# Cross-attention with a norm: v made one batch later and kept in PSUM, transposed contexts kept for four batches, contexts loaded flat for the bound

## The reference, cut to what matters

```python
# x: (16, 512, 512), ctx: (16, 120, 256); Wq (512,512), Wk, Wv (256,512)
q = x @ Wq + bq                       # (16, 512, 512)
k = ctx @ Wk + bk                     # (16, 120, 512)
v = ctx @ Wv + bv                     # (16, 120, 512)
w = softmax((q @ k^T) / sqrt(512), axis=1)    # over the 512 tokens
y = w @ v + x
out = (y - mean(y)) * rsqrt(var(y) + 1e-6) * gamma + beta
```

## Time and profile before

| | |
|---|---|
| median of 3 runs | 225.95 us (225.01 to 226.12) |
| the profiled execution | 226.4 us, span 224.6 us |
| PE busy | 193.4 us |
| DVE busy | 174.2 us |
| POOL busy | 167.6 us |
| ACT busy | 162.0 us |

### The profile page before, as it was taken

How to read it: one execution, slowest core, us unless ns; L and a number is a source line. 1 busy time by engine, 2 the same in 40 slices (tenths; PEclk the granted TensorE clock), 3 DMA queues, 4 the chain that set the end, 5 groups by cost and what they waited for, 6 DMA issues and landing times.

```text
span 224.6 us, 4180 instructions
## 1 busy us (share of the span) xinstructions
PE 193.4 (86%) x1168; PEld 119.5 (53%) x1168; DVE 174.2 (78%) x435; ACT 162.0 (72%) x343; POOL 167.6 (75%) x164
## 2 busy tenths in 40 slices
PE   5698599999999999999999999999999999988000
PEld 4554567656657564657474646565655556524000
DVE  0482855698989598879695988796968899869993
ACT  2426467589898788787887988887969897886610
POOL 1000000438999999999999999999999999999792
PEclk9799889999999999999999999999999999999755
DMA  5999966001464656373636473646455544040454
GB/s 152 303 233 327 352 240 233 0 4 53 181 228 171 188 209 210 144 245 150 235 161 220 175 232 163 223 172 220 175 209 187 198 177 187 0 190 0 188 211 163
DMA packets 11914, 41.04 MB, mean 183 GB/s; under 512 B 1022, under 2 KB 5886, under 8 KB 8062
## 3 DMA queue, kind: packets, MB, share of 16 engines
q1 hardware_dynamic: 11614, 40.37, 50.9%
q10 hardware_dynamic: 288, 0.52, 1.0%
HBM read 24.12 MB, written 16.78 MB: 182 GB/s over the span
## 4 chain that ended last, share of the span: by engine, by line
POOL 60%; issue 10%; DMA 9%; PE 7%; DVE 6%; ACT 2%; DVEq 1%; SPq 1%; POOLq 1%; ACTq 0%
POOL obuf L959 22%; POOL obuf L953 20%; DMA obuf<-in_ctx 7%; POOL rstd L986 6%; POOL v_part L946 6%; POOL square_mean L972 4%; PE g_ps L395 2%; DMA out<-obuf 2%; PE s_ps L425 2%; DVE obuf L822 1%; DVEq L78 1%; PE v_ps L384 1%; POOL var_eps L979 1%; POOL var_eps L976 1%; PE xT_ps L403 1%
## 5 line engine op out<-in xcount | busy, mean ns | idle before, releaser
L953 POOL TENSOR_TENSOR obuf<-obuf,gamma_all 128x512 f32<-128x512 f32 x44 | 57.8, 1338 | 1.5 <-ACT obuf L617 1.5
L425 PE MATMUL s_ps<-xT,gT 128*120 128x512 f32 x128 | 57.8, 593 | 1.1 <-ACT xT L554 1.1
L959 POOL TENSOR_TENSOR obuf<-obuf,beta_all 128x1536 f32<-128x1536 f32 (+1 forms) x16 | 51.8, 3238 | 1.2
L617 ACT ACTIVATE obuf<-xbuf,shift,rstd 128x512 f32<-128x512 f32 x44 | 32.7, 804 | 15.1 <-POOL shift L991 15.1
L417 PE MATMUL pv_ps<-v_part,prob_part 120*128 120x512 f16 x135 | 35.6, 380 | 3.0 <-issue 1.4
L425 PEld LDWEIGHTS s_ps<-xT,gT 128*120 128x120 f32 x128 | 23.2, 183 | 27.2 <-issue 21.1
L403 PEld LDWEIGHTS xT_ps<-ident,xbuf 128*128 128x128 f32 x256 | 30.0, 143 | 13.1 <-issue 8.1
L403 PE MATMUL xT_ps<-ident,xbuf 128*128 128x128 f32 x256 | 34.3, 278 | 1.8 <-ACT xT L554 1.4
L554 ACT ACTIVATE xT<-xT_ps 128x512 f32<-128x512 f32 x64 | 34.1, 584 | 1.3 <-PE xT_ps L403 1.3
L833 DVE SCALAR_TENSOR_TENSOR xbuf<-pv_ps,back_y,xbuf 128x512 f32<-128x512 f32 x45 | 32.4, 743 | 0.8 <-POOL shift L991 0.6
L946 POOL TENSOR_TENSOR v_part<-v_scaled,v_part 120x512 f16<-120x512 f32 x16 | 21.5, 1344 | 13.6 <-ACT v_part L587 13.1
(11 more groups left out here) (119 smaller groups left out, 260.2 us busy)
## 6 DMA issues: line engine op xcount, KB each, us to landing
xbuf<-in_x SPq DMA_DIRECT2D x16, 1024.0 KB, 4.8
out<-obuf SPq DMA_DIRECT2D x14, 1024.0 KB, 4.2
out<-obuf SPq DMA_DIRECT2D x8, 256.0 KB, 2.4
ctx_nat<-in_ctx SPq DMA_DIRECT2D x16, 120.0 KB, 4.2
obuf<-in_ctx SPq DMA_DIRECT2D x2, 960.0 KB, 14.9
wq_nat<-in_L_xattn_Wq SPq DMA_DIRECT2D x2, 512.0 KB, 8.6
wk_nat<-in_L_xattn_Wk SPq DMA_DIRECT2D x1, 512.0 KB, 5.7
wv<-in_L_xattn_Wv SPq DMA_DIRECT2D x1, 512.0 KB, 12.6
```

The source lines that it names most:

```text
L425: mm = pe.matmul(s_ps[0:M, :], gT[:, k % 2, e, :], xT[:, e, :], start=(e == 0), stop=(e == EC - 1))
L617: act.activation(obuf[:, k % 2, j, :], xbuf[:, kn, j, :], ACT.Identity, bias=shift[:, j:j + 1], scale=rstd[:, k % 2, j:j + 1]).then_inc(no ...
L953: pool.tensor_tensor(obuf[:, k % 2, j, :], obuf[:, k % 2, j, :], gamma_all[:], ALU.mult)\
L959: done = pool.tensor_tensor(obuf[:, k % 2, 0:share, :], obuf[:, k % 2, 0:share, :], beta_all[:].unsqueeze(1).broadcast_to([P, share, E]), ...
```

## The change

v of batch b is made in slot b, no longer in slot b-1. It stays in its PSUM bank (v_ps; pv_ps[0] for batch 0): DVE scales it in place (`scale_v`), ACT takes the high half out of PSUM, behind `probs_to_high`, and DVE takes the low half (`v_to_low`), behind `probs_to_low`. POOL has no part in v. `ctxT` has four places. PE's product 2 waits for `v_low` where it waited for `v_copied`. `key_bias` of batches 1 and 2 moves into slot 1, and the low half of Wv behind `key_bias` of batch 0. `ctx_all` is loaded as one flat block over 128 partitions, 15,360 bytes in each, in two transfers (2048 and 1792 columns); ACT adds up two parts of 1024 columns, DVE two of 1024 and 768, and the last two of DVE's four dot products with Wq move behind these. An assertion on sizes changes as well and is left out here.

```diff
@@ -121,14 +121,13 @@
         ctx_nat = sb("ctx_nat", [M, RING, L + 1])
-        ctxT = sb("ctxT", [P, 2, 2, LC, M], F16)
+        ctxT = sb("ctxT", [P, RING, 2, LC, M], F16)
         xbuf = sb("xbuf", [P, RING, RJ, E])
...
         prob_part = sb("prob_part", [M, 2, T], F16)
-        v_scaled = sb("v_scaled", [M, 2, E])
         v_part = sb("v_part", [M, 2, 2, E], F16)
@@ -161,7 +160,9 @@
-        ctx_all = obuf[0:M].rearrange("m q j e -> m (q j e)")[:, 0:B * L]
+        CTX_COLS = B * M * L // P
+        CTX_EDGES = [-(-h * CTX_COLS // L // CTX_PARTS) * L for h in range(CTX_PARTS + 1)]
+        ctx_all = obuf[:].rearrange("p q j e -> p (q j e)")[:, 0:CTX_COLS]
@@ -258,6 +259,10 @@
+        def v_bank(b):
+
+            return pv_ps[0] if is_slot(b, 0) else v_ps
+
@@ -283,11 +288,10 @@
             load_ctx(0, 0)
-            all_v = ctx_all.rearrange("m (b l) -> m b l", l=L)
+            flat = ctx_in.rearrange("b m l -> (b m l)").rearrange("(p q) -> p q", p=P)
             for h in range(2):
-                sp.dma_start(all_v[:, h * B // 2:(h + 1) * B // 2],
-                             ctx_in[h * B // 2:(h + 1) * B // 2].rearrange("b m l -> m b l"))\
-                    .then_inc(ctx_all_in[h], 16)
+                q = slice(CTX_EDGES[h * CTX_PARTS // 2], CTX_EDGES[(h + 1) * CTX_PARTS // 2])
+                sp.dma_start(ctx_all[:, q], flat[:, q]).then_inc(ctx_all_in[h], 16)
             load_x(0, 0)
@@ -367,7 +371,7 @@
                 if is_in(b, 2, B):
-                    pe.wait_ge(key_done, max(b, 3) if isinstance(b, int) else b)
+                    pe.wait_ge(key_done, 1 if is_slot(b, 2) else b)
                 pe.wait_ge(ctx_loaded[k], 16 * (r + 1))
@@ -375,13 +379,11 @@
                 pe.wait_ge(ctx_low, b + 1)
-                if is_in(b, 1, B):
-                    pe.wait_ge(v_copied, b)
-                if is_in(b, 3, B):
-                    pe.wait_ge(y_done, RJ * (b - 3) + 3)
+                if is_in(b, 2, B):
+                    pe.wait_ge(y_done, RJ * (b - 2) + 3)
                 steps = [(c, *parts) for c in range(LC) for parts in PASSES]
                 for n, (c, of_ctx, of_w) in enumerate(steps):
-                    mm = pe.matmul(v_ps[0:M, :], ctxT[:, k % 2, of_ctx, c, :], wv_part[:, of_w, c, :],
+                    mm = pe.matmul(v_bank(b)[0:M, :], ctxT[:, k % RING, of_ctx, c, :], wv_part[:, of_w, c, :],
                                    start=(n == 0), stop=(n == len(steps) - 1))
@@ -393,7 +395,7 @@
                         mm = pe.matmul(g_v[:, e, :], qk_part[:, of_w, c, e * P:(e + 1) * P],
-                                       ctxT[:, k % 2, of_ctx, c, :], start=(n == 0), stop=(n == len(steps) - 1))
+                                       ctxT[:, k % RING, of_ctx, c, :], start=(n == 0), stop=(n == len(steps) - 1))
                 mm.then_inc(g_done, 1)
@@ -407,8 +409,8 @@
                     pe.wait_ge(y_done, RJ * b)
-                if j == 2 and is_in(b, 0, B - 2):
-                    pe.wait_ge(v_copied, b + 3)
+                if j == 2 and is_in(b, 0, B - 1):
+                    pe.wait_ge(v_low, b + 2)
                 if j == 3 and is_in(b, 0, B - 1):
@@ -473,17 +475,13 @@
                     turn_x(s, k, 1)
-                if is_slot(s, 1):
-                    context_v(1, 1)
-                elif more:
-                    context_v(s + 1, k1)
+                if main:
+                    context_v(s, k)
                 if main:
...
                     context_g(s + 1, k1)
-                if is_slot(s, 1):
-                    context_v(2, 2)
                 if is_slot(s, B - 1):
@@ -494,13 +492,13 @@
                     pe.wait_ge(prob_high, s)
-                    product(s - 1, k + 1, 0)
-                    product(s - 1, k + 1, 1)
-                    product(s - 1, k + 1, 2)
+                    product(s - 1, k - 1, 0)
+                    product(s - 1, k - 1, 1)
+                    product(s - 1, k - 1, 2)
                 if is_in(s, 0, B - 2):
...
                 if last:
-                    product(s - 1, k + 1, 3)
+                    product(s - 1, k - 1, 3)
                 if main and not is_slot(s, B - 1):
@@ -521,7 +519,6 @@
                            accum_out=own_bound[:, WK:WK + 1]).then_inc(act_bounds, 1)
-            part = B * L // CTX_PARTS
@@ -531,23 +528,23 @@
                 act.wait_ge(ctx_all_in[h * 2 // CTX_PARTS], 16)
-                act.activation(act_junk[0:M, h * part:(h + 1) * part], ctx_all[:, h * part:(h + 1) * part], ACT.Abs,
-                               accum_out=own_bound[0:M, h:h + 1]).then_inc(act_bounds, 1)
+                part = slice(CTX_EDGES[h], CTX_EDGES[h + 1])
+                act.activation(act_junk[:, part], ctx_all[:, part], ACT.Abs,
+                               accum_out=own_bound[:, h:h + 1]).then_inc(act_bounds, 1)
...
             copy_wqT(1)
+            copy_wqT(2)
             sum_ctx(0)
-            copy_wqT(2)
+            copy_wqT(3)
             sum_ctx(1)
-            copy_wqT(3)
-            sum_ctx(2)
...
                 act.wait_ge(ctx_turned, b + 1)
-                if is_in(b, 2, B):
-                    act.wait_ge(g_done, b - 1)
-                act.activation(ctxT[:, k % 2, HIGH], ctxT_v, ACT.Copy, scale=scale[:, 0:1]).then_inc(ctx_high, 1)
+                if is_in(b, RING, B):
+                    act.wait_ge(v_copied, b - RING + 1)
+                act.activation(ctxT[:, k % RING, HIGH], ctxT_v, ACT.Copy, scale=scale[:, 0:1]).then_inc(ctx_high, 1)
@@ -580,14 +577,12 @@
-                def v_to_high(b, parity):
+                def v_to_high(b, k):
                     act.wait_ge(v_copied, b + 1)
...
                         act.wait_ge(pv_done, RJ * (b - 1))
-                    act.activation(v_part[:, parity, HIGH], v_scaled[:, parity], ACT.Copy).then_inc(v_high, 1)
-
-                if is_in(s, 2, B):
-                    v_to_high(s, k % 2)
+                    act.activation(v_part[:, k % 2, HIGH], v_bank(b)[0:M, :], ACT.Copy).then_inc(v_high, 1)
+
@@ -620,10 +615,11 @@
                     if is_slot(s, 1):
+                        v_to_high(0, 0)
                         ctx_to_high(2, 2)
                     probs_to_high(s - 1)
-                if is_slot(s, 1):
-                    v_to_high(0, 0)
+                if main:
+                    v_to_high(s, k)
                 if is_slot(s, B - 1):
@@ -632,8 +628,6 @@
                     copy_xT(s, 3)
-                if is_slot(s, 1):
-                    v_to_high(1, 1)
                 if is_in(s, 1, B - 2):
@@ -689,12 +683,14 @@
             largest(own_bound[:, WQ:WQ + 1], wq_nat[:].rearrange("p c e -> p (c e)"))
-            for c in range(EC):
+            for c in range(EC // 2):
                 dot(LC + c, wq_nat[:, c], bk_all, u_col[:, c:c + 1])
             dve.wait_ge(ctx_all_in[1], 16)
-            dve.tensor_reduce(own_bound[0:M, CTX_PARTS - 1:CTX_PARTS],
-                              ctx_all[:, (CTX_PARTS - 1) * B * L // CTX_PARTS:], AX.X, ALU.add,
-                              apply_absolute_value=True).then_inc(dve_bounds, 1)
+            for h in range(2, CTX_PARTS):
+                dve.tensor_reduce(own_bound[:, h:h + 1], ctx_all[:, CTX_EDGES[h]:CTX_EDGES[h + 1]],
+                                  AX.X, ALU.add, apply_absolute_value=True).then_inc(dve_bounds, 1)
+            for c in range(EC // 2, EC):
+                dot(LC + c, wq_nat[:, c], bk_all, u_col[:, c:c + 1])
             dve.wait_ge(w_spread, 1)
@@ -732,7 +728,7 @@
                 dve.wait_ge(ctx_high, b + 1)
-                dve.scalar_tensor_tensor(ctxT[:, k % 2, LOW], ctxT_v, scale[:, 0:1], ctxT[:, k % 2, HIGH],
+                dve.scalar_tensor_tensor(ctxT[:, k % RING, LOW], ctxT_v, scale[:, 0:1], ctxT[:, k % RING, HIGH],
                                          ALU.mult, ALU.subtract).then_inc(ctx_low, 1)
@@ -745,7 +741,7 @@
             dve.tensor_copy(bound[:, 2:3], max_bound[:, WV:WV + 1])
-            dve.wait_ge(dve_bounds, 4)
+            dve.wait_ge(dve_bounds, 5)
             scales(dve.scalar_tensor_tensor(bound[:, 3:4], bound[:, 0:1], max_bound[:, WV:WV + 1], bv_bound[:],
@@ -755,8 +751,6 @@
             dve.tensor_tensor(onto_v[:], back_v[:], scale[:, 3:4], ALU.mult)
-            low_part(wv_part[:, LOW], wv[:], scale[:, 2:3], wv_part[:, HIGH], 3)
-            dve.wait_ge(low_split, 3)
@@ -767,14 +761,17 @@
             key_bias(0, 0, 0)
-            key_bias(1, 1, 0)
-
-            def copy_v(b, k):
+            low_part(wv_part[:, LOW], wv[:], scale[:, 2:3], wv_part[:, HIGH], 3)
+
+            def scale_v(b):
                 dve.wait_ge(v_done, b + 1)
-                if is_in(b, 2, B):
-                    dve.wait_ge(v_low, b - 1)
-                dve.scalar_tensor_tensor(v_scaled[:, k % 2], v_ps[0:M, :], onto_v[0:M, :], bv_scaled[0:M, :],
+                dve.scalar_tensor_tensor(v_bank(b)[0:M, :], v_bank(b)[0:M, :], onto_v[0:M, :], bv_scaled[0:M, :],
```

(38 more changed lines are left out.)

## The result

217.84 us median of 4 runs (217.75 to 218.16) against 226.03 of the kernel before (4 runs, 225.01 to 226.25): ratio 0.9663, 95% interval 0.9623 to 0.9703. The profiled execution took 218.16, span 216.4; against before's 226.4 and 224.6 the span is 8.2 shorter. That is the quantity taken apart here.

The account below looks back on a forecast made before the run. POOL and PE, nearly full, were taken to bound the kernel, tied by waits through ACT and DVE. From 226.4, -1.1 - 0.2 + 0.7 - 3.0 + 0.4 = -3.2 gave 223.2; the median, 0.45 lower, made it 222.8 (219.3 to 227.6).

Parts of the forecast that it names:

- The start: Up to the first scale (L721): ctx_all lands at 17.7, scale at 21.2; gain 1.1, from loss 1.6 to gain 1.8.
- my bound of 3.4: Load of ctx_all: the most its landing could come sooner, with 371 GB/s held; 2.7 was taken.
- Rival 2: Load of ctx_all: gains only by the count of engines, landing 0.5 sooner; total 225.0, chance 0.18.
- Slot 1: PE loses a v product, DVE gets more work: 1.3 off, 1.1 back, gain 0.2 (-0.6 to +1.0).
- Slot 2: L617 comes 0.7 later with nothing saved before it: loss 0.7 (0 to 0.8).
- The slots: Slots 2 to 15: period falls from 11.38 to 11.15 (bounds 10.8 and 11.6), 3.0 us gained over 13.
- Both rings: In a slot, the ACT-and-DVE cycle and POOL's cycle: both predicted to close at 11.05 to 11.15.
- L815 "waits 0.35": DVE's center in each slot: ready at A+9.65, A being L604's start, held by POOL's L959 until A+10.0.
- POOL's 1.16: L946, v's low half, taken off POOL: worth 0.3 a slot for POOL alone, up to 0.75 where DVE held it.
- Rival 3: Slots: rescale L822 falls behind POOL's L953, 0.45 on the ring, slot 11.6; total 228.7, chance 0.17.
- The tail: Last batch: scores wait longer for ACT (+0.6), POOL's chain +0.15; loss 0.4 taken (0.1 to 0.7).
- Rival 4: Slots: holds fall away, POOL idle while L822 runs, ring 10.8; total 218.2, chance 0.09.

Follow-up runs that it names:

- e5: Changed kernel with ctx_all loaded over 128 partitions in 1 KB rows instead of long flat runs: 218.93 us against 224.76 of the kernel before.
- e6: Changed kernel with ctx_all loaded flat over 120 partitions, 4096 columns each, instead of 128 partitions: 224.51 us against 224.53 of the kernel before.
- e1: Kernel before with only the flat load of ctx_all, its sums and the order of the dots: 221.85 us against 224.70.
- e2: Changed kernel with the old load of ctx_all, old sums and dots: 222.76 us against 224.70 of the kernel before.
- e3: Kernel before with 15 identity transposes filling PE's gap ahead of the first g: 224.43 us against 224.70, no difference.
- e4: Changed kernel, ACT copying only two columns of v's high half from batch 2 on: 220.41 us, 0.9808 of the kernel before.
- e7: Changed kernel with a dummy subtract on POOL at the removed one's place, slots 2 to 15: 221.49 us against 224.76 of the kernel before.
- e14: e1 with v's low half moved from POOL to DVE, v still early and in SBUF: 223.32 us against 224.53 of the kernel before.
- e11: e8 and e4's edit together: 214.13 us against 224.76 of the kernel before.
- e8: Changed kernel with DVE's rescale put ahead of v's low half: 215.21 us against 224.76 of the kernel before.
- e12: e10 with all slots written out, no hardware loop: 213.81 us against 224.53 of the kernel before.
- e10: e8 with all four dots ahead of the wait for ctx_all: 214.93 us against 224.53 of the kernel before.

## Why the prediction was wrong in size

- **The start: the term was mis-sized.** The forecast had the load land at 17.7 and the first scale at 21.2, a gain of 1.1. They came at 16.16 and 19.44, a gain of 2.9, outside the bound of 1.8. The serial work behind the landing was nearly as forecast (3.28 against 3.5). What failed is the speed: 340 GB/s was taken, "a tenth under x", where 418 stands in the rows; and landing 4.3 sooner lies beyond my bound of 3.4, because 371 GB/s was taken as the ceiling although wq's row had 384. Rival 2, which let the load gain no more than the count of engines (0.5 sooner), didn't hold: by e5 and e6 the partitions are the cause, at 3.7 to 4.4 us of landing. By e1, 0.6 of the 2.9 came only because PE ran at 1.00 from 9 to 15 us, which the prediction didn't consider.
- **TensorE's clock: no term for it.** 1.7 of the 1.9 us between first scale and slot 2 is g and eight transposes at a granted clock of 0.50 in before's profiled execution. The page's clock row and g's 2.46 stood there to be read; a sum made against one execution has to ask whether a stretch of it ran at the lower level. The profiled executions of e2 and e3 run without it.
- **Slot 1**: 0.2 forecast; 0.2 is what is left of the 1.9, so nothing speaks against it, but no run tests it by itself.
- **Slot 2** was right: +0.7 forecast, +0.7 measured.
- **The slots: the mechanism was right, the period was not.** Both rings had closed at 11.05 to 11.15, and 11.15 was taken "for a slot in which L822 loses now and then". It never lost: 0.74 in slots 2 to 15. Measured 11.03, 4.5 us instead of 3.0. The steps behind it held: subtract 0.69 (0.67 taken), copy 0.60 (0.6), POOL idle 0.93 and more ahead of gamma, released by ACT (0.9), the three gammas at 4.2 where the rescale is 0.1 ahead of gamma, and down to 3.85 where it is 0.5 ahead. Of L815 "waits 0.35" at most 0.31 was seen (0.74 to 1.06). The leads repeat from one loop turn to the next, so a mixture of slots that win and slots that lose, from which the 11.15 was taken, didn't come about: in after the rescale starts ahead of gamma in every slot, in e4 behind it in every slot from 2 to 14.
- **What POOL's 1.16 is worth** was forecast at 0.3 for POOL alone; e7 says 0.26, its hold of the rescale included. But the ring's gain as a whole depends on the order as well, which the prediction treated as a risk and never as part of the gain: e14 moves the same work without that order and gains nothing.
- **Rival 3** (slower) named a real mechanism and the right point of decision, a lag of 0.1 us. Its price, 0.45 a slot, was too high as far as the runs tell: over slots 2 to 14 e4 and e11 (10.72), which differ in the order alone, are 0.41 apart, but after and e8 (10.77) are 0.22 apart by the same swap without any loss behind gamma, which leaves about 0.2 for falling behind (an estimate from these four; ACT's full copy with the rescale behind gamma was never run). By the Trainium skill, "SBUF — State Buffer", section "Who interferes with whom", the one to start first has the shared ports for its whole length: e4's 1.63, with gamma 0.18 ahead, and e8's 0.74 agree.
- **The tail**: 0.4 forecast, 0.4 measured, and that is partly luck. The last scores were to wait longer for ACT than before's 1.11; in after they start at 188.57 and run 3.94 with no such wait. What ACT's copy costs there shows earlier, in the 11.56 from slot 14 to 15, and the 2.84 of the last center, which was to stay, fell to 1.89.
- **Rival 4** named 218.2, near the measured 217.84, for a ring of 10.8. That ring wasn't there (11.03), so the agreement is luck; e8 (10.82) and e11 (10.75) made it afterwards.

Forecast -3.2, measured -8.2: 1.8 of the difference from the load, 1.7 from the clock at g, 1.5 from the period.

## What to carry to other kernels

When DVE instructions with two SBUF operands meet GpSimd's, don't only count busy time: find which starts first in each turn, and put DVE's into the hole in which GpSimd waits for a third engine. Two swapped calls were worth 2.6 us here, and less work on ACT alone cost 2.6, as it turned that order round (medians of different chips; 3.0 and 2.3 between the profiled spans). Load a large tensor that is only summed over all 128 partitions, whatever its own shape. Before an edit is priced by one profiled execution, look for stretches at the lower clock level in it.

## What the runs showed of the hardware that was not expected

- A load of 120 partitions ran at 220 (1 KB rows, before) and 229 GB/s (long rows, e6) in the window at 13 to 14 us, and one of 128 at 351 (1 KB rows, e5) and 418 (long rows, after).
- Work taken off one engine can lengthen the kernel: ACT's copy from 0.60 to 0.17 us a slot cost 2.6 us (e4).
- The turn of the hardware loop of four slots costs about 0.6 us (11.24 to 11.27 for 10.63 to 10.69, e8); written out it is gone (10.68 to 10.70, e12), 1.1 us over the kernel.
- The granted clock at the start differs between executions: g took 2.46 at 0.50 (before) or 1.42 at 1.00 (after, e2, e3). In seven of the fourteen profiled executions, before, e1, e3, e5, e6, e12 and e14, the clock was 0.50 in a stretch from 9 us on, to 12 in before and to about 15 in the others; in each of them PE had stood idle for most or all of the window at 8 to 9 us, and in the other seven it hadn't. e12, at 0.50 at 12 to 13 us, has its first scale at 20.17, where e10 with the same start in its code has 18.92 at 1.00; e12's profiled execution came 1.4 above its median.
